# Loading the last stage's first tile inside the attention stage, and two buffers for attended values

## The reference

```
q = x @ Wqkv[:, :1024]   (32 heads of 32);  k, v = one shared head of 32 each
scores = q k^T / sqrt(32) + slope[h] * (pos_k - pos_q), causal
attn   = softmax(scores) v;   attn = attn @ Wo
x = layernorm(x + attn)
w_q = int4 fake quantization of weight in groups of 128
out = layernorm(x + x @ w_q^T + bias)
```

## Time and profile before

| | us |
|---|---|
| median of three runs | 2506.91 |
| lowest, highest | 2504.71, 2510.05 |
| the profiled execution, its own time | 2510.49 |
| its span, from first to last instruction | 2508.8 |
| PE busy | 2327.9 (93%) |
| DVE busy | 1634.3 (65%) |
| ACT busy | 1016.1 (41%) |
| mean granted TensorE clock | 0.97 of full speed |

### The profile page before, as it was taken

How to read it: one execution, slowest core, us unless ns; L and a number is a source line. 1 busy time by engine, 2 the same in 40 slices (tenths; PEclk the granted TensorE clock), 3 DMA queues, 4 the chain that set the end, 5 groups by cost and what they waited for, 6 DMA issues and landing times. The chain is left out here.

```text
span 2508.8 us, 37558 instructions
## 1 busy us (share of the span) xinstructions
PE 2327.9 (93%) x12576; PEld 1534.6 (61%) x12576; DVE 1634.3 (65%) x4666; ACT 1016.1 (41%) x1944; POOL 913.6 (36%) x563
## 2 busy tenths in 40 slices
PE   5999999699999999999999999994899999999998
PEld 4777777454444444444444444441788888888886
DVE  5777667487677777777677677771455565556554
ACT  3222222166666666666666666663110111111110
POOL 0000000036676776766676676774011011110110
PEclk8999999879999999999999999997999999999999
DMA  5445554563323323313313313304333323333330
GB/s 202 164 163 178 190 182 149 146 195 86 73 57 85 76 56 86 82 49 86 81 49 86 81 49 86 82 15 175 108 101 97 89 83 100 100 81 92 94 100 26
DMA packets 176808, 255.85 MB, mean 102 GB/s; under 512 B 15118, under 2 KB 104846, under 8 KB 176162
## 3 DMA queue, kind: packets, MB, share of 16 engines
q1 hardware_dynamic: 176674, 254.18, 35.1%
HBM read 166.04 MB, written 87.03 MB: 101 GB/s over the span
## 5 line engine op out<-in xcount | busy, mean ns | idle before, releaser
L947 DVE CUSTOM_DVE_ANT_0 unused<-pa,distance 128x512 bf16<-128x512 f32 (+3 forms) x1536 | 776.7, 553 | 326.6 <-PE pa L784 323.2
L923 ACT ACTIVATE probs<-pa,slope 128x512 f32<-128x512 f32 (+3 forms) x1536 | 780.4, 583 | 388.8 <-PE pa L807 383.1
L763 POOL TENSOR_TENSOR probs<-probs 128x1024 f32<-128x1024 f32 (+2 forms) x256 | 679.7, 2655 | 125.9 <-ACT probs L923 109.3
L784 PE MATMUL pa<-k,ff_hi 96*128 96x512 f32 (+1 forms) x1008 | 360.6, 390 | 37.9 <-DMA slope<-in_c_slope 24.7
L821 PE MATMUL pa<-probs,v 128*32 128x512 f32 (+3 forms) x3072 | 329.0, 500 | 21.3 <-DVE att L967 13.2
L784 PEld LDWEIGHTS pa<-k,ff_hi 96*128 96x128 f32 x1008 | 192.3, 195 | 230.0 <-DVE mx L947 134.6
L1164 POOL TENSOR_TENSOR yb<-y,bias 128x1024 f32<-128x1024 f32 x32 | 77.4, 2420 | 670.0 <-DVE z L1187 631.5
L807 PE MATMUL pa<-ff_hi,k 116*128 116x512 f32 (+1 forms) x798 | 315.8, 411 | 0.0
L749 POOL TENSOR_SCALAR_AFFINE_SELECT probs<-probs 128x512 f32<-128x512 f32 x256 | 162.7, 636 | 282.5 <-ACT probs L923 280.9
L295 PE MATMUL ps<-xt_hi,wq_hi 128*128 128x512 f32 (+1 forms) x576 | 230.0, 399 | 26.5 <-DVE wq_lo L392 15.4
L1074 PE MATMUL pf<-fo_hi,at_hi 128*128 128x512 f32 x512 | 203.7, 398 | 34.5 <-DVE at_lo L1179 34.5
(11 more groups left out here) (110 smaller groups left out, 2931.3 us busy)
## 6 DMA issues: line engine op xcount, KB each, us to landing
ff_hi<-q_hi_d SPq DMA_DIRECT2D x84, 256.0 KB, 4.7
x_in<-in_L_attn_hidden_states SPq DMA_DIRECT2D x8, 2048.0 KB, 8.6
q_hi_d<-q_hi SPq DMA_DIRECT2D x64, 256.0 KB, 2.0
q_lo_d<-q_lo SPq DMA_DIRECT2D x64, 256.0 KB, 2.3
att_d<-att SPq DMA_DIRECT2D x64, 256.0 KB
at_in<-att_d SPq DMA_DIRECT2D x32, 512.0 KB, 4.3
recip<-recip_d SPq DMA_DIRECT2D x128, 128.0 KB, 5.7
x_in<-in_L_attn_hidden_states SPq DMA_DIRECT2D x32, 512.0 KB, 8.0
```

Of the source, the lines that this page charges most:

```text
L763: nc.gpsimd.tensor_tensor(o, o, probs[:, source % PR, h0:h1, 0:N], ALU.add).then_inc(add_done, 1)
L784: nc.tensor.matmul(bank[:, 0:keys], q3[u][0:3 * D, qb // BPH, h, qb % BPH * P:(qb % BPH + 1) * P], k3[u][0:3 * D, k0:k0 + keys], start=Tru ...
L923: nc.scalar.activation(probs[:, n % PR, h, 0:N], sc_ps[sc_ring.bank[use]][:, at:at + N], ACT.Exp, scale=slope[:, bass.ds(g * HPG + h, 1)]) ...
L947: nc.vector.tensor_tensor_reduce(out=unused[:, mx_ring.bank[n], 0:keys], in0=bank[:, 0:keys], in1=distance[:, d0:d0 + keys], scale=1.0, sc ...
```

## The change

In `attend`'s last iteration, behind the store of the first half, SP now waits for the inverted `early`, stores it to `recip_d`, waits for that store, and loads the attended values and the reciprocals of tile 0 into buffers that outlive the stage (`at_first`, `recip_first`). Behind the loop, `late` is only read back; the stage ends without waiting for it. DVE inverts `late` in `finish`, behind the split of tile 0, and SP stores it there.

In `finish`, `at_in` and `recip` have two buffers each, with a semaphore each. SP's order is now: attended values and reciprocals of tile 1, x of tile 0, identity, bias, a quarter of `wf_lo`, the late reciprocals' store; then in turn 0, once `at_lo` of tile 0 is done, x of tile 1, attended values and reciprocals of tile 2, the rest of `wf_lo`, and a wait for both stores of reciprocals. In turn t it loads x of tile t+1 and attended values and reciprocals of tile t+2. PE waits for identity and bias between h0 and h1 of tile 0, no longer ahead of everything.

```diff
@@ layer
+        at_first = ctx.enter_context(nc.sbuf_tensor("at_first", [P, KT, P], fp32))
+        recip_first = ctx.enter_context(nc.sbuf_tensor("recip_first", [P, KT, P], fp32))
+        late = ctx.enter_context(nc.sbuf_tensor("late", [P, P], fp32))
+        at_loaded = [ctx.enter_context(nc.semaphore(f"at_loaded{n}")) for n in range(2)]
+        late_in, recip_stored = (ctx.enter_context(nc.semaphore(n)) for n in ("late_in", "recip_stored"))
@@ attend
-        late_d = [d[EARLY:ITS].rearrange("t h (a q) -> (t h a) q", q=P) for d in (sums_d, recip_d)]
+        late_d = sums_d[EARLY:ITS].rearrange("t h (a q) -> (t h a) q", q=P)
...
                 put_att(sp, t, 0)
+                if last:
+                    sp.wait_ge(recip_done, 1)
+                    sp.dma_start(early_d[1], early[:, :]).then_inc(recip_stored, 16)
+                    sp.wait_ge(recip_stored, 16)
+                    load_attended(sp, att_d, recip_d, at_first, recip_first, at_loaded[0], 0)
...
             put_att(sp, ITS - 1, 1)
             for c in range(HALF):
                 sp.wait_ge(att_stored[c], 32 * ITS + CREDIT)
-            sp.dma_start(late[:, :], late_d[0]).then_inc(sums_back, 16)
-            sp.wait_ge(recip_done, 1)
-            sp.dma_start(early_d[1], early[:, :]).then_inc(recip_stored, 16)
-            sp.wait_ge(recip_done, 2)
-            sp.dma_start(late_d[1], late[:, :]).then_inc(recip_stored, 16)
-            sp.wait_ge(recip_stored, 32)
+            sp.dma_start(late[:, :], late_d).then_inc(late_in, 16)
...
             evacuate(ITS - 1, 1)
-            dve.wait_ge(sums_back, 32)
-            nc.vector.reciprocal(late[:, :], late[:, :]).then_inc(recip_done, 1)
+def load_attended(sp, att_d, recip_d, at_in, recip, loaded, t):
+
+    sp.dma_start(at_in[:, :, :], att_d[:, :, bass.ds(t * P, P)].rearrange("g p q -> p g q")).then_inc(loaded, 16)
+    b, at = t // (S // P), (t % (S // P)) * P
+    for h in range(HPG):
+        src = recip_d[bass.ds(b * NG, NG), h, bass.ds(at, P)]
+        sp.dma_start(recip[h * D:(h + 1) * D, :, :], src[None, :, :].to_broadcast([D, NG, P])).then_inc(loaded, 16)
@@ finish
-        at_in = sb("at_in", [P, KT, P])
-        recip = sb("recip", [P, KT, P])
+        at_in = [at_first, sb("at_in", [P, KT, P])]
+        recip = [recip_first, sb("recip", [P, KT, P])]
...
+            load_at(1, 1)
+            load_x(0, 0)
+            sp.dma_start(ident[:, :], ident_h).then_inc(consts_in, 16)
             sp.dma_start(bias[:, :], bias_h[None, :].to_broadcast([P, H])).then_inc(consts_in, 16)
-            sp.dma_start(ident[:, :], ident_h).then_inc(consts_in, 16)
...
-            load(0, 0)
-            sp.dma_start(raw(wf_lo[:, :, :]), wf_d[1]).then_inc(wf_lo_in, 16)
+            load_wf(0, KT // 4)
+            sp.wait_ge(late_done, 1)
+            sp.dma_start(recip_d[B * NG - 4:B * NG].rearrange("t h (a q) -> (t h a) q", q=P), late[:, :]).then_inc(recip_stored, 16)
 
             def body(t, u, i):
...
                 if not last:
                     sp.wait_ge(at_lo_done, t + 1)
-                    load(t + 1, 1 - u)
+                    load_x(t + 1, 1 - u)
+                if not last and not before_last:
+                    load_at(t + 2, u)
+                if first:
+                    load_wf(KT // 4, KT)
+                    sp.wait_ge(recip_stored, 32)
@@ finish, tensor
-                    pe.wait_ge(wf_lo_in, 16)
+                    pe.wait_ge(wf_lo_in, 32)
...
-            pe.wait_ge(consts_in, 32)
             pe.wait_ge(w3_in[0], 16)
             pe.wait_ge(w3_in[1], 16)
...
                 product(o_ps, o_done, at, (wo_hi, wo_lo), 0)
-                if not first:
+                if first:
+                    pe.wait_ge(consts_in, 32)
+                else:
                     turn(t - 1, 1 - u)
                 product(o_ps, o_done, at, (wo_hi, wo_lo), 1)
@@ finish, vector
-            def normalize(t):
-                dve.wait_ge(at_loaded, (t + 1) * 16 * (1 + HPG))
-                nc.vector.tensor_tensor(at_in[:, :, :], at_in[:, :, :], recip[:, :, :], ALU.mult).then_inc(at_norm, 1)
+            def normalize(t, u, i):
+                dve.wait_ge(at_loaded[u], i * (16 * (1 + HPG)) + 16 * (1 + HPG))
+                nc.vector.tensor_tensor(at_in[u][:, :, :], at_in[u][:, :, :], recip[u][:, :, :], ALU.mult).then_inc(at_norm, 1)
...
-            normalize(0)
+            normalize(0, 0, 0)
             split_lo(0, 0)
+            dve.wait_ge(late_in, 16)
+            nc.vector.reciprocal(late[:, :], late[:, :]).then_inc(late_done, 1)
```

More of the change, by code:

```diff
@@ L152, in layer @@
         w3_in = [ctx.enter_context(nc.semaphore(n)) for n in ("fo_hi_in", "fo_lo_in", "ff_hi_in")]
+        at_first = ctx.enter_context(nc.sbuf_tensor("at_first", [P, KT, P], fp32))
[3 more added lines that the diff above has]
+        late_in, recip_stored = (ctx.enter_context(nc.semaphore(n)) for n in ("late_in", "recip_stored"))
         attend(nc, distance, qrows, krows, ident_h, slope_h, q_hi_d, q_lo_d, k_d, v_d, att_d, sums_d, recip_d,
-               wo_d, wf_d, w3, w3_in)
-        finish(nc, x, bias, ident_h, att_d, recip_d, wf_d, w3, w3_in, out)
+               wo_d, wf_d, w3, w3_in, at_first, recip_first, at_loaded, late, late_in, recip_stored)
+        finish(nc, x, bias, ident_h, att_d, recip_d, wf_d, w3, w3_in, at_first, recip_first, at_loaded, late, late_in, recip_stored, out)
 def project(nc, x, wqkv, wo, wf, qscale_h, ident_h, q_hi_d, q_lo_d, k_d, v_d, wo_d, wf_d):
@@ L521, in attend @@
 def attend(nc, distance_h, qrows_h, krows_h, ident_h, slope_h, q_hi_d, q_lo_d, k_d, v_d, att_d, sums_d, recip_d,
-           wo_d, wf_d, w3, w3_in):
+           wo_d, wf_d, w3, w3_in, at_first, recip_first, at_loaded, late, late_in, recip_stored):
     ITS = B * NG
@@ L639, in attend @@
         EARLY = ITS - 4
-        early, late = sb("early", [EARLY * HPG, S]), sb("late", [P, P])
+        early = sb("early", [EARLY * HPG, S])
         psum = [ctx.enter_context(nc.psum_tensor(f"pa{n}", [P, CH], fp32)) for n in range(8)]
@@ L652, in attend @@
         pv_done, att_done, sums_done, add_done = sem("pv_done"), sem("att_done"), sem("sums_done"), sem("add_done")
-        sums_back, recip_done, recip_stored = sem("sums_back"), sem("recip_done"), sem("recip_stored")
+        sums_back, recip_done = sem("sums_back"), sem("recip_done")
         att_stored = [sem(f"att_stored{c}") for c in range(HALF)]
@@ L989, in _, with finish @@
             evacuate(ITS - 1, 1)
-            dve.wait_ge(sums_back, 32)
-            nc.vector.reciprocal(late[:, :], late[:, :]).then_inc(recip_done, 1)
-def finish(nc, x, bias_h, ident_h, att_d, recip_d, wf_d, w3, w3_in, out):
+def load_attended(sp, att_d, recip_d, at_in, recip, loaded, t):
[4 more added lines that the diff above has]
+        sp.dma_start(recip[h * D:(h + 1) * D, :, :], src[None, :, :].to_broadcast([D, NG, P])).then_inc(loaded, 16)
+def finish(nc, x, bias_h, ident_h, att_d, recip_d, wf_d, w3, w3_in, at_first, recip_first, at_loaded, late, late_in, recip_stored, out):
     NT = T // P
@@ L1027, in finish @@
         consts_in, wf_lo_in, at_norm = sem("consts_in3"), sem("wf_lo_in"), sem("at_norm")
-        at_loaded, x_loaded = sem("at_loaded"), [sem(f"x3_loaded{n}") for n in range(2)]
+        late_done, x_loaded = sem("late_done"), [sem(f"x3_loaded{n}") for n in range(2)]
         at_hi_done, at_lo_done = sem("at_hi_done"), sem("at_lo_done")
@@ L1037, in _, with load_at, load_x, load_wf @@
         def _(sp):
-            sp.dma_start(bias[:, :], bias_h[None, :].to_broadcast([P, H])).then_inc(consts_in, 16)
-            sp.dma_start(ident[:, :], ident_h).then_inc(consts_in, 16)
[L1040 to L1046, removed]
-            load(0, 0)
-            sp.dma_start(raw(wf_lo[:, :, :]), wf_d[1]).then_inc(wf_lo_in, 16)
+            def load_at(t, u):
+                load_attended(sp, att_d, recip_d, at_in[u], recip[u], at_loaded[u], t)
+            def load_x(t, u):
+                sp.dma_start(x_in[:, u:u + 1, :], x_v[:, bass.ds(t, 1), :]).then_inc(x_loaded[u], 16)
+            def load_wf(k0, k1):
+                sp.dma_start(raw(wf_lo[:, k0:k1, :]), wf_d[1, :, k0:k1, :]).then_inc(wf_lo_in, 16)
+            load_at(1, 1)
+            load_x(0, 0)
+            sp.dma_start(ident[:, :], ident_h).then_inc(consts_in, 16)
+            sp.dma_start(bias[:, :], bias_h[None, :].to_broadcast([P, H])).then_inc(consts_in, 16)
+            load_wf(0, KT // 4)
+            sp.wait_ge(late_done, 1)
+            sp.dma_start(recip_d[B * NG - 4:B * NG].rearrange("t h (a q) -> (t h a) q", q=P), late[:, :]).then_inc(recip_stored, 16)
             def body(t, u, i):
                 first, last = isinstance(t, int) and t == 0, isinstance(t, int) and t == NT - 1
+                before_last = isinstance(t, int) and t == NT - 2
                 if not last:
                     sp.wait_ge(at_lo_done, t + 1)
-                    load(t + 1, 1 - u)
+                    load_x(t + 1, 1 - u)
```

(13 more changed lines are left out.)

## The result

The changed kernel takes 2492.47 us (median of 4 runs, 2491.49 to 2494.69) against 2508.48 (4 runs): ratio 0.994, interval 0.9922 to 0.9957, so 16.0 us faster. Run again beside other kernels it gave 0.9938 (0.9924 to 0.9951). The forecast was 18.4 us faster, which from the earlier median of 2506.91 made 2488.5; the measured time lies 4.0 above that, 2.4 from the smaller gain and 1.6 because the kernel before came out slower here.

What follows compares the result with a forecast made beforehand. Last stage bound by PE from its second tile on, so tile 1's earlier start decides: 18.9 less 0.5 for the clock is 18.4 us, from median 2506.91 to 2488.5 us; range 2484.0 to 2495.6.

Steps and rivals of the forecast that it cites:

- The place: Last stage: PE runs without a wait from tile 1 to the tail, so an earlier start there shortens the kernel equally.
- The stage's end and tile 0: Attention's end: next stage begins 4.1 us earlier, tile 0's loads are hidden, and PE starts tile 0 18.9 us earlier.
- The wait for the constants: Between tile 0's halves: identity and bias, behind tile 1's loads, land at 1748.0 and stall PE 3.1 us (0 to 4.7).
- The rival with no stall: Inside tile 0: constants land in time, tile 1 starts 3.1 us sooner, kernel takes 2485.4 us; chance 0.18.
- Tile 1: PE starts tile 1 at 1758.6 against 1777.45, 18.9 us earlier; the new buffer takes its load off this path.
- The clock: Around tile 1: pause of 3.1 leaves the clock up, 5.1 doesn't; 0.5 us added, bounds -1.6 and +2.6.
- The weights: Ahead of `linear(0)`: data including the larger part of `wf_lo` land by 1765.7 us, cover 6.9; no stall taken.
- the full queue: Rival ahead of `linear(0)`: PE stalls 5.5 us for `wf_lo`, low clock adds 1.6, kernel takes 2495.6 us; chance 0.15.
- The entry: Rival at the last stage's entry: an engine waits for instructions, work begins up to 4.0 us late; 2492.5 us, chance 0.08.

## Why the prediction held, point by point

**The place.** Shown: PE has no wait between tile 1 and the tail, before or after, so the first tiles decide. From ACT's last copy to the first `linear` the change saves 15.7 and 17.8 in its two profiles; the medians say 16.0 and 15.5. The profiled execution's span of 2489.8 lies only 0.6 from the forecast 2490.4, but that is luck: 2.3 of its 19.0 us are the difference of runs ahead of the change.

**The stage's end and tile 0.** The entry is 3.7 sooner (forecast 4.1: from SP's last issue to the next stage's first it took 0.66, from 1731.10 to 1731.76, and not 0.38), and putting the late inversion back costs 4.0 at tile 0. The store of the early reciprocals and the five loads cost nothing, with tile 0's loads issued from 1715.22. Tile 0 starts on PE 18.7 sooner (forecast 18.9). Shown.

**The wait for the constants.** Forecast: bias 14.3 after the entry and a stop of 3.1. Measured: 1745.95 - 1731.76 = 14.2, a stop of 2.6 and, again, 1.1. That the queue ahead is its cause is shown by the kernel with the constants first. The rival with no stall is refuted for this kernel; it is what the moved wait and the other order bring about. The constants did not overtake the reciprocals, the last of which landed 9.4 after its issue, near 1743.2. But the order of landing is not the order of issue throughout: identity, issued at 1734.79 behind x at 1734.29, landed near 1744.3, 0.2 ahead of x. Both in one view (KB, us to landing):

```profile
x_in<-in_L_attn_hidden_states SPq DMA_DIRECT2D x1, 512.0 KB, 10.2
ident<-in_c_ident SPq DMA_DIRECT2D x1, 64.0 KB, 9.5
```

Bias landed behind both, so the stall doesn't hang on this.

**Tile 1.** It was said that the second buffer takes tile 1's load off the path. It does, and the wait for `at_lo` is the 5.1 worked out. What the prediction did not put together is that this same load is what makes bias late: one buffer ends up in nearly the same place.

**The clock.** This term was mis-sized: 0.5 with bounds of -1.6 and +2.6. I let a pause of 3.1 leave the clock up. It fell behind a pause of 2.6 (8 matmuls 0.43 apart, 1.9 us), behind one of 2.1 in another kernel, and not behind one of 1.1. Tile 1's first half took 8.32 where 7.6 was forecast, 1.2 more than before. The term thus measured 1.9 + 1.2 = 3.1 in the first profile, beyond its bound, and 1.5 in the second, where the clock did not fall between the halves. That tile 0's first half took 0.4 more than before cost nothing, since PE then waited for bias. The first `linear` came 2.6 later than forecast (0.3 at the second half's start, 1.8 from there to tile 1, 0.5 behind), nearly the whole distance between 18.4 and 15.7; in the second profile 17.8 were saved. The tail gave 1.0 back, 9 slow matmuls instead of 13 behind the same pause of 4.8, which the change did not touch: luck of the run.

**The weights.** No wait for `ff_lo`. Its larger part, issued at 1748.83, landed 16.3 later, +37.2 (forecast +35.5), 7.8 ahead of need. The two kernels with PE busy and x loaded in the last stage start `linear` when it lands, at +38, so the full queue is a bound that lies just behind, and was none here.

**The entry.** No engine waited behind it for anything not shown: `normalize(0)` starts at 1731.70. That rival is refuted, and with it the reading of the Trainium skill's page "Runtime: NRT & Kernel Launch", section "Instruction fetch mechanics", as a stall in this place; no row shows how far code had been fetched.

## What to carry to other kernels

When a load is pulled ahead at the start of a stage, look at what it now stands in front of in its queue: here tile 1's data delayed a bias that PE asked for earlier than it needed it, and moving the wait to the first use was worth as much as the order of the loads. Parts of a change that remove waits one behind the other do not add up, so time each alone. Price short waits of TensorE with the low clock behind them, 0.2 us for each 512-column matmul that runs slowly.

## What the runs showed of the hardware

- The granted clock came down behind pauses of 2.6 and 2.1 us, 3.5 us after PE had stopped and with PE working again, and stayed up behind the one of 1.1. These are three profiles of one execution each, and the delay differs elsewhere: in the tail's pause of 4.8 it came down 3.9 us after PE had stopped in the kernel before, and 2.2 after (2464.83 to 2467.06) in the changed one, whose mean granted clock in this half microsecond is 0.56:

```profile
2467.00:2467.50 0.50, 0.00 (x0) 0.00 (x0) 0.43 (x3) 0.04 (x1) 0.17 (x1) 0.56 0.00 0
```

- In each low stretch at a restart 6 to 14 matmuls of 512 columns ran 0.43 instead of 0.23 us apart, in all profiles here, which alone is 1.2 to 2.8 us. With three such stretches this can make part of the runs' spread; that it does is not shown.
- Matmuls that nobody reads kept the clock up in the pauses that they filled, and slowed nothing that could be seen: tile 0 starts at +7.4 to +7.7 with them and at +7.6 without, and 20 of them won 2.0 us at the tail.
- With much queued, issuing itself takes long. The four reciprocal loads that SP issues in 2.06 us at the entry of the changed kernel took this in the same stage, behind 4.2 MB issued since the entry, a part of it landed by then:

```profile
1742.50 6.28 SPq L1005 DMA_DIRECT2D recip_first<-recip_d  x4
```

In other places with little or nothing queued they took 1.8 to 3.4 (3.35 at 1777.86 in the kernel before), and 4.9 to 11.1 with the loads of the stage's start under way. That fits the queue as the cause, but no run isolates it.
